# The stage between two attentions: output projections and norms first, then rotation, transposition and key products in a staggered order over six PSUM banks

## What is computed

```python
x = layernorm(x + attention_1(x) @ Wo + bo)          # closes the first attention
xh = x.reshape(1, 2048, 16, 8)
r1 = xh[..., 0::2] * cos - xh[..., 1::2] * sin       # rotation by position
r2 = xh[..., 0::2] * sin + xh[..., 1::2] * cos
q_in = k_in = interleave(r1, r2)
q = q_in @ Wq.T + bq                                 # only the first block of queries here
k = k_in @ Wk.T + bk
v = x @ Wv.T + bv                                    # in the following stage, from x transposed
scores = causal(q k / sqrt(8)); softmax; times v; ...
```

## Time and profile before

| | |
|---|---|
| time, median of 3 runs | 1837.18 us (1836.56 to 1837.46) |
| the profiled execution | 1835.85 us, of which the span of the trace is 1834.1 us |
| busy share of the span | PE 92%, DVE 69%, ACT 65%, POOL 10% |
| mean granted clock of PE | 0.958 of full speed |
| the changed stage | from 774.8 us to 832.5 us of the span, 57.7 us |

### The profile page before, as it was taken

One profiled execution on the slowest core, in us unless ns is written; L12 is line 12 of the kernel. 1 busy time (PEld: TensorE's weight loads), 2 busy tenths in 40 slices (PEclk: granted clock), 3 DMA queues, 4 the chain that ended last, 5 costly groups with the idle time before them and its releaser, 6 DMA issues. The chain is left out here.

```text
span 1834.1 us, 25946 instructions
## 1 busy us (share of the span) xinstructions
PE 1683.9 (92%) x10028; PEld 795.2 (43%) x10028; DVE 1263.6 (69%) x1804; ACT 1194.6 (65%) x2436; POOL 182.9 (10%) x171
## 2 busy tenths in 40 slices
PE   6999999999999999749999999999886699699997
PEld 3433333333333333235444444455554466344443
DVE  4888888888888887046888677675375276255555
ACT  4588888888888888735677777777546564333332
POOL 1000000000000000130000000111245000100100
PEclk9899999999999999979899999999988799699999
DMA  1000000000000000010000000000100000212220
GB/s 61 1 1 1 1 1 1 1 1 1 1 1 1 1 1 1 20 28 1 1 1 1 1 1 1 1 1 2 36 1 0 12 1 1 106 60 93 98 84 26
DMA packets 7274, 29.98 MB, mean 16 GB/s; under 512 B 680, under 2 KB 2736, under 8 KB 4848
## 3 DMA queue, kind: packets, MB, share of 16 engines
q1 hardware_dynamic: 7152, 28.33, 4.2%
HBM read 27.15 MB, written 1.18 MB: 15 GB/s over the span
## 5 line engine op out<-in xcount | busy, mean ns | idle before, releaser
L879 DVE TENSOR_REDUCE a_part_max<-a_ps 128x2 f32<-128x1024 f32 x512 | 602.3, 1220 | 87.1 <-PE a_ps L681 86.5
L864 ACT ACTIVATE a_probs<-a_ps 128x512 f32<-128x512 f32 x1024 | 533.2, 613 | 131.0 <-PE a_ps L777 128.6
L879 DVE TENSOR_REDUCE f_part_max<-f_ps 128x2 f32<-128x1024 f32 (+3 forms) x320 | 327.7, 1061 | 121.3 <-PE f_ps L681 65.3
L777 PE MATMUL a_ps<-a_q_shift,a_KA 64*128 64x512 f32 x1024 | 367.7, 448 | 3.8 <-POOL a_q_shift L660 2.6
L864 ACT ACTIVATE f_probs<-f_ps 128x512 f32<-128x512 f32 (+3 forms) x640 | 300.2, 538 | 99.8 <-PE f_ps L781 48.6
L777 PEld LDWEIGHTS a_ps<-a_q_shift,a_KA 64*128 64x128 f32 x1024 | 166.4, 187 | 291.4 <-ACT a_probs L864 275.5
L681 PE MATMUL a_ps<-a_KA,a_q_open 64*128 64x512 f32 x1024 | 277.7, 468 | 4.4 <-DVE a_part_max L879 3.7
L795 PE MATMUL a_psO<-a_probs,a_VA 128*32 128x512 f32 x2048 | 275.6, 610 | 3.9 <-ACT a_probs L864 3.9
L777 PE MATMUL f_ps<-f_q_shift,f_KA 64*128 64x512 f32 (+3 forms) x640 | 224.1, 435 | 4.8 <-POOL f_q_shift L660 2.2
L681 PE MATMUL f_ps<-f_KA,f_q_open 64*128 64x512 f32 (+3 forms) x640 | 170.3, 430 | 5.2 <-DVE f_part_max L879 4.4
L777 PEld LDWEIGHTS f_ps<-f_q_shift,f_KA 64*128 64x128 f32 x640 | 106.3, 188 | 150.2 <-ACT f_probs L864 138.5
(11 more groups left out here) (321 smaller groups left out, 1780.3 us busy)
## 6 DMA issues: line engine op xcount, KB each, us to landing
t_c_all<-c_rows SPq DMA_DIRECT2D x16, 1024.0 KB, 8.0
experts_w<-in_experts SPq DMA_DIRECT2D x1, 3264.0 KB, 10.3
W<-in_weights SPq DMA_DIRECT2D x1, 1574.0 KB, 6.3
out<-X SPq DMA_DIRECT2D x4, 256.0 KB, 6.9
K<-in_consts SPq DMA_DIRECT2D x1, 644.0 KB, 7.0
R<-in_rows SPq DMA_DIRECT2D x1, 530.0 KB, 6.0
W<-in_weights SPq DMA_DIRECT2D x1, 512.0 KB, 6.8
mx_conv_rows<-in_conv_rows SPq DMA_DIRECT2D x1, 512.0 KB, 4.1
```

Of the source, the lines that this page charges most:

```text
L777: mm = pe.matmul(bank(r)[:, lo:512], g.KA[rows, 2 * n + jp, P * s:P * s + P], q_shift[rows, u % 2, jp, lo:512], start=True, stop=not diag)
L864: nc.scalar.activation(probs[:, st % 2, j, lo:512], bank(r)[:, lo:512], ACT.Exp, scale=SCALE).then_inc(ring_read, 1)
L879: dve.tensor_reduce(part_max[:, 4 * q + 2 * jp:4 * q + 2 * jp + 2, c], ps1[:, k % 2, :, 0:b - a], AX_X, ALU.max).then_inc(max_read, 1)
```

## The change

Nothing is added or taken out: each engine executes the same instructions with the same shapes (PE 3552, DVE 778, ACT 502 rows of the program's listing in both). Their order inside the stage changes, and the banks.

- PE does all four `heads`, `turn_a` and `project_out` first, with `turn_x(0)` between; then the pieces of `items`, in the order r0 x1 k0 r1 x2 k1 r2 x3 k2 r3 k3 q.
- The ring has six banks, 6, 7, 0, 1, 2, 3. Before the third piece (x1, bank 0) PE waits that the fourth `normalized` has read banks 0 to 3.
- ACT does `copy_at` and `apply1` first, then the same list; `apply1(3)` stands behind `copy_x(1)` and ahead of `high(("k", 0))`. `fill_spread`, four small copies that stood last in the stage, stands behind `copy_at(1)`.
- DVE's `rope_right` is cut in two (`rope_right`, `rope_sum`), and its order is new. POOL's order is the same.

```diff
-        items, banks = [], (6, 7) if tail else tuple(range(8))
+        items, banks = [], (6, 7, 0, 1, 2, 3) if tail else tuple(range(8))
         if tail:
...
-            items = [("x", 0)]
-            for b in range(1, NB):
-                items += [("r", b - 1), ("k", b - 1), ("x", b)]
-            items += [("r", NB - 1), ("k", NB - 1), ("q", first)]
+            items = [("x", 0), ("r", 0), ("x", 1), ("k", 0), ("r", 1), ("x", 2), ("k", 1), ("r", 2), ("x", 3), ("k", 2),
+                     ("r", 3), ("k", 3), ("q", first)]
...
                     k = items.index(one)
+                    if tail and k == 2:
+                        pe.wait_ge(a_done, NB)
...
                     if b + 1 < NB:
                         heads(b + 1)
-                    if b >= 2:
-                        turn_r(b - 2)
-                        project(("k", b - 2))
                     project_out(b)
-                    if b:
-                        turn_x(b - 1)
...
+                    if b == 2:
+                        turn_x(0)
+                for kind, b in items[1:]:
...
                         copy_at(b)
-                        if b >= 2:
-                            copy_r(b - 2)
-                            high(("k", b - 2))
+                        if b == 1:
+                            act.wait_ge(sel_clear, 1)
+                            fill_spread(g, g.k_spread, K_PARTS, sel_in)
+                        if b == NB - 1:
+                            copy_x(0)
                         if b:
                             apply1(b - 1)
...
+                        if (kind, b) == ("x", 1):
+                            apply1(NB - 1)
...
                     if b + 1 < NB:
                         normalized(b + 1)
-                    if b >= 2:
-                        split(("k", b - 2))
                     if b:
                         mean1(b - 1)
+                    if b == NB - 1:
+                        rope_right(0)
+                        rope_sum(0)
                     residual(b)
-                    if b:
-                        rope_right(b - 1)
+                rope_right(1)
+                rope_sum(1)
                 mean1(NB - 1)
-                split(("k", NB - 2))
-                rope_right(NB - 1)
-                split(("k", NB - 1))
+                rope_right(2)
+                split(("k", 0))
+                rope_sum(2)
+                split(("k", 1))
+                rope_right(3)
+                rope_sum(3)
+                split(("k", 2))
+                split(("k", 3))
                 split(("q", first))
```

More of the change, by code:

```diff
@@ L225, in front_stage @@
         kq.insert(NB if tail else 2, ("q", first))
-        items, banks = [], (6, 7) if tail else tuple(range(8))
+        items, banks = [], (6, 7, 0, 1, 2, 3) if tail else tuple(range(8))
         if tail:
-            for b in range(NB):
-                items += [("x", b)]
-                if b:
-                    items += [("r", b - 1), ("k", b - 1)]
-            items += [("r", NB - 1), ("k", NB - 1), ("q", first)]
-            order = [("x", 0), ("r", 0), ("k", 0), ("x", 1)]
-            items = [("x", 0)]
-            for b in range(1, NB):
-                items += [("r", b - 1), ("k", b - 1), ("x", b)]
-            items += [("r", NB - 1), ("k", NB - 1), ("q", first)]
+            items = [("x", 0), ("r", 0), ("x", 1), ("k", 0), ("r", 1), ("x", 2), ("k", 1), ("r", 2), ("x", 3), ("k", 2),
+                     ("r", 3), ("k", 3), ("q", first)]
         else:
@@ L356, in _ @@
                         heads(b + 1)
-                    if b >= 2:
-                        turn_r(b - 2)
-                        project(("k", b - 2))
                     project_out(b)
-                    if b:
-                        turn_x(b - 1)
[L363 to L368, removed]
+                    if b == 2:
+                        turn_x(0)
+                for kind, b in items[1:]:
+                    if kind == "x":
+                        turn_x(b)
+                    elif kind == "r":
+                        turn_r(b)
+                    else:
+                        project((kind, b))
             @block.scalar
@@ L403, in _ @@
                         copy_at(b)
-                        if b >= 2:
-                            copy_r(b - 2)
-                            high(("k", b - 2))
+                        if b == 1:
[3 more added lines that the diff above has]
+                            copy_x(0)
                         if b:
                             apply1(b - 1)
[L409 to L416, removed]
+                    for kind, b in items[1:]:
+                        if kind == "x":
+                            copy_x(b)
+                        elif kind == "r":
+                            copy_r(b)
+                        else:
+                            high((kind, b))
+                        if (kind, b) == ("x", 1):
+                            apply1(NB - 1)
                 else:
@@ L422, in _ @@
                             high(one)
-                act.wait_ge(sel_clear, 1)
-                fill_spread(g, g.k_spread, K_PARTS, sel_in)
+                    act.wait_ge(sel_clear, 1)
+                    fill_spread(g, g.k_spread, K_PARTS, sel_in)
             @block.vector
@@ L476, in rope_right, with rope_sum @@
                     dve.tensor_tensor(pair(XR)[:, :, 1:2], pair(g.X)[:, :, 0:1], pair(SN)[:, :, 1:2], ALU.mult).then_inc(sw_right, 1)
+                def rope_sum(b):
                     dve.wait_ge(sw_right, b + 1)
```

1 line of the change is left out of this document (removed).

## The result

| | before | after |
|---|---|---|
| median | 1837.18 us (1834.95 to 1841.81, 17 runs) | 1819.28 us (1814.74 to 1834.67, 17 runs) |
| ratio | | 0.9908, 95% interval 0.9893 to 0.9923 |
| profiled execution, its span | 1835.85 us, 1834.1 us | 1819.28 us, 1817.5 us |
| mean granted clock of PE | 0.958 | 0.962 |
| PE's first transposition of the stage to the end of the last `split` | 57.37 us | 40.26 us |

The account below looks back on a forecast made before the run. A chain hopping between engines, none full, was taken to bound the stage. Its end, 832.19, moves to 810.5, plus 3.75 net of new waits to 814.3, or 818.0 at half clock; middle gain 16.0 gives 1821.2 us, range 1817.4 to 1825.0.

Parts of the forecast that it names:

- The chain: In the changed stage, written order alone makes block b+1's norm wait for block b-1's key product; one turn 12.3 us.
- The walk without waits of a new kind: New order's steps to the last split: end at 810.5, 21.7 us before 832.19.
- The new wait: DVE and POOL instructions with two SBUF inputs hold each other, five times in the chain: 4.05 us, net 3.75.
- The sum of block 1 behind POOL's power for block 3: DVE's sum of block 1 waits for POOL's power in the stage: 0.7 us.
- The rule of the Trainium skill: Lock extends to two-port tensor_scalar, so block 0's cut also waits behind POOL: end 814.5 instead of 814.3.
- The sum at full clock: Last split of the stage ends at 814.3, 17.9 us early, if PE keeps full clock.
- The clock: PE idles in the stage, so half clock from about 793 on; end at 818.0 instead of 814.3.
- The middle: Stage's gain taken between 17.9 and 14.2 us early: 16.0 us.
- The edits costed at nothing: Moving fill_spread, the wait for normalized(3) ahead of bank 0, and six banks in the stage: no cost.
- DVE and POOL don't hold each other: Rival: no new wait in the stage; gain 21.7 us at full clock, 18.1 at half; chance 0.10.
- DVE loses both products in a row: Rival: DVE waits for both POOL products each time, 2.5 us worse than the middle, 1823.7 us; chance 0.12.
- The slower rival: Half clock outlives the stage; 32 us longer cancels the 16 us gain, 45 more gives 1843.7 us; chance 0.02.

Follow-up runs that it names:

- e9: Kernel after, with POOL waiting at five places for DVE instructions and PE's idle places filled with transpositions: stage 36.05 us, median 1814.28 us.
- e5: Kernel after, with POOL's two rotation products per block replaced by constant writes, so those products are left out: stage 36.20 us, median 1811.27 us.
- e4: Kernel after, with 76 unread transpositions added where PE waits in the stage: stage 38.89 us, median 1815.68 us.
- a0_after_again: Kernel after, run again with no edit as the reference: stage 42.05 us, median 1820.44 us.
- e7: Kernel after, with ACT's fill_spread back at the end of its order: stage 39.90 us, median 1817.55 us.
- e6: Kernel before in its old order, with the six-bank ring and the wait for bank 0: ratio 0.9997, stage 57.60 us.
- e2: Kernel after, with the old ring of two banks and no wait ahead of bank 0: stage 42.70 us, median 1820.95 us.
- e3: Kernel after, with each block's x, r and k pieces together on PE and ACT, not staggered: stage 39.00 us, median 1820.62 us.
- e8: Kernel after, with POOL's rotation products waiting for the next block's f_minus_mean and PE's idle places filled: stage 37.07 us, median 1814.37 us.
- e10: Kernel after, with each block's pieces together, not staggered, and PE's idle places filled: stage 38.30 us, median 1815.99 us.

## Why the prediction was right

- **The chain.** Right. The order of the engines had held the norms, and they now run through: block 3's norm starts on ACT at 800.43 (801.5 forecast; the stage began 0.4 us early, and 0.7 is the term that failed, below). The walk without waits of a new kind ended at 810.5, a stage of 810.5 - 774.8 = 35.7 us (its own steps, 797.9 and 12.8, add up to 810.7). e9, with the five waits gone, two smaller ones new and the clock full, has 36.05; e5, where POOL reads nothing in its products, 36.20.
- **The new wait.** Right in its mechanism, with one term of five wrong. `mean1(1)`, `mean1(2)`, the sum of block 0 and `mean1(3)` were put at 0.7, 1.0, 0.55 and 1.1 us more; they show 0.85 - 0.15 = 0.70, 1.22 - 0.15 = 1.07, 1.22 - 0.69 = 0.53, and 1.23 - 0.15 = 1.08. "The sum of block 1 behind POOL's power for block 3 (0.7)" failed: it took its plain 0.69 us. The wait was derived from products of 1.27 and 0.43 us and carried over to a power of 1 us on four values a partition. In every profile of the new order the sum of block 1 takes 0.69 us. So that power does not hold DVE for its length. It is itself 0.1 us longer (1.11) behind DVE's half rotation, as the rule has it; the prediction counted three such powers as free of that in the new order, and only two are, so 0.2 and not 0.3 us was won back.
- **The rule of the Trainium skill.** Right, and it beat the rows. "SBUF — State Buffer", section "Who interferes with whom", has `tensor_scalar` in a two-port mode take part in the lock; the prediction set it beside the sum at +0.2 us at the end. The cut of block 0 took 1.02 instead of 0.43 us behind POOL's product of block 3, and moving that product behind it (e9) was part of a gain of 1.02 us. The same section says that POOL's pure writes don't hold a DVE instruction with two SBUF inputs; e5 agrees (0.16 us beside a write of 0.52), while the cut was 0.10 us longer beside a write.
- **The sum at full clock.** Forecast 814.3 - 774.8 = 39.5 us; e4 measured 38.89 at a clock of 1.00. Without the term that failed it would be 38.8. The lock as a whole was put at 3.75 net; e4 to e9 measured 38.89 - 36.05 = 2.84, where 3.75 - 0.7 = 3.05 was left; that e9 also frees the cut and brings two waits of its own makes the closeness partly luck.
- **The clock.** Right as a range. Half clock was expected "from about 793 on"; it is there at 791.97. But it did not last: r1 and x2 ran at full clock again, and of the seven pieces from k1 on only k1, r2, x3 and k2 were slow. So two of the signs missed: the granted clock in 796 to 806 was 0.67, not near 0.5, and the fourth output projection ended at 794.03 instead of 793.7, slowed to 2.06 us. It cost 40.26 - 38.89 = 1.4 us in the first profile and 42.05 - 38.89 = 3.2 us in the second; the range had 0 to 3.7. The middle, 16.0 us of gain, stands between the 17.1 and 15.3 that the two profiles show; nothing in the prediction chose it but the two ends, so how near it came is luck. The start of the next stage was left unchanged, and in the first profile it is (0.62 and 0.62); a0_after_again has 3.4 us more at half clock there.
- **The edits costed at nothing** cost nothing: `fill_spread` (e7), and six banks were never awaited in the old order (e6). In the new order they are worth up to 2.8 us of the stage (e2), where the prediction gave them no value of their own.
- **The rivals.** That DVE and POOL don't hold each other fell with the first `f_minus_mean`; that DVE loses both products in a row did not occur (none of the three took more than 1.23 us). The slower rival, a half clock that outlives the stage, exists but falls short: in e3 the half clock in the next stage lasted 27 us longer than in the kernel after (some 31 against 3.4) and cost 11.4 us, where 32 us and 16 us would have been needed. Each us at half clock cost 0.42 us, not 0.5. The two runs of the kernel after at 1833.5 and 1834.7 us had a clock of 0.954 and 0.952, and fit the same event; they have no profile, so that is inferred. Its chance of 0.02 was low for a single run (2 of 17 came within the 0.2% of no change, none was slower), not for the median.

Not settled is why e3's long half clock came in that run. The four filled runs of that order were without it, which may be chance, and that is all that is known.

## What to carry to other kernels

Where the busy time of every engine is far below the stage's length, follow one turn of the loop from engine to engine and ask of each wait whether the data or only the written order makes it: here the new order gave 14.7 us of 57 with the old banks (e2), and more PSUM banks without the new order did nothing (e6). Some of that gain is clock (3 to 4 us, an estimate). When a reordering puts DVE beside POOL, look for short DVE instructions with two SBUF inputs behind long POOL products, and let the short one go first, with a wait if need be: five such waits took 2.8 us off a stage of 38.9 at full clock. And where PE idles inside a chain (2.25 and 3.03 us here), filler transpositions in the idle places kept the clock at full in the profiles of all four kernels that had them, worth 1.4 and 3.2 us of the stage against the two profiles of the kernel after. Whether they also narrow the spread of the runs is not shown. The two together (e9) are 5 us below the kernel after by the medians, 1814.28 against 1819.28, and their ratios to before don't overlap (0.9859 to 0.9889 and 0.9893 to 0.9923).

## What the runs showed of the hardware

- PE stayed at half clock while it was busy for 27.62 of 27.80 us (e3), with four products at 2.07 us instead of 1.20. Being fully busy did not bring the full clock back for some 31 us in that run, while in the two profiles of the kernel after it came back some 4 and 8 us into the next stage. The Trainium skill, "TensorE: Matmul & The Clock Gate", Part 1, has the clock rise once PE has been busy; this run went against it, and the measurement decides.
- With transpositions of a constant tile in its idle places PE stayed at 1.00 throughout the stage in the profiles of e4, e8, e9 and e10.
- `f_minus_mean`, with two SBUF inputs, ends 0.01 or 0.02 us behind the POOL product that it starts behind (0.15 us become 0.85 and 1.22), and beside a POOL write of 0.52 us it keeps its 0.16 us. DVE's cut of 128x512 (`TENSOR_SCALAR`, one SBUF input) goes from 0.43 to 1.02 us behind a POOL product and to 0.53 us beside a write that has 0.25 us left (e5).
- A POOL power on four values a partition, 1.0 us long, is delayed 0.1 us by a DVE instruction with two SBUF inputs, but DVE's sum runs beside it in its plain 0.69 us.
- The time of one and the same kernel follows the granted clock: the 17 runs of the kernel after go from 1814.7 us at 0.967 to 1834.7 us at 0.952.
